# Down-bias sums of the first stage: from VectorE additions to TensorE identity products with ScalarE copies

## The reference, cut to what matters

```python
combine = combine.at[jnp.arange(N)[:, None], topk_idx].set(topk_w)
...
out = jnp.einsum('nei,edi->ned', act, down_proj) + down_proj_bias
y = jnp.einsum('ned,ne->nd', out, combine.astype(out.dtype))
...
x = x + _L0_attn_ref(xn, ...) + _L0_ffn_ref(xn, ...)
```

## Time and profile before

| | |
|---|---|
| median of 3 runs | 3066.34 us (3065.47 to 3067.68) |
| profiled execution, its time | 3062.34 us |
| profiled execution, its span | 3060.4 us |
| PE busy / PE weight loads busy | 2769.5 us / 2259.8 us |
| DVE, ACT, POOL busy | 2129.6, 1627.7, 1437.1 us |
| mean granted PE clock | 0.968 |

### The profile page before, as it was taken

One profiled execution on the slowest core, in us unless ns is written; L12 is line 12 of the kernel. 1 busy time (PEld: TensorE's weight loads), 2 busy tenths in 40 slices (PEclk: granted clock), 3 DMA queues, 4 the chain that ended last, 5 costly groups with the idle time before them and its releaser, 6 DMA issues. The chain is left out here.

```text
span 3060.4 us, 61227 instructions
## 1 busy us (share of the span) xinstructions
PE 2769.5 (90%) x20990; PEld 2259.8 (74%) x20990; DVE 2129.6 (70%) x6019; ACT 1627.7 (53%) x3420; POOL 1437.1 (47%) x2201
## 2 busy tenths in 40 slices
PE   5878799999999999979999999999799999999995
PEld 3655588898889889756666666666688888888864
DVE  5788788788778778767788888866544445444565
ACT  3555444544544444556656656665455555555563
POOL 4475843443453444365556665332333323333487
PEclk8888899999999999999999999999999999999998
DMA  3566678888789788422434443210566666566445
GB/s 84 203 233 241 219 278 296 293 296 309 280 290 325 276 296 309 153 45 54 100 99 108 110 111 105 95 70 26 210 228 208 211 204 238 204 215 208 138 89 127
DMA packets 212006, 580.12 MB, mean 190 GB/s; under 512 B 24616, under 2 KB 146416, under 8 KB 167408
## 3 DMA queue, kind: packets, MB, share of 16 engines
q1 hardware_dynamic: 172528, 523.82, 48.8%
q0 software_dynamic: 36864, 51.14, 8.2%
q10 hardware_dynamic: 2304, 1.21, 0.1%
HBM read 450.14 MB, written 125.96 MB: 188 GB/s over the span
## 5 line engine op out<-in xcount | busy, mean ns | idle before, releaser
L494 PE MATMUL bank<-xh,gu 128*128 128x256 f32 x3520 | 672.5, 291 | 34.2 <-DVE gc L1683 26.1
L1154 POOL TENSOR_TENSOR al<-t,ah 128x512 fp32r<-128x512 f32 x220 | 283.2, 1287 | 875.5 <-ACT ah L1388 875.5
L494 PEld LDWEIGHTS bank<-xh,gu 128*128 128x128 f32 x3520 | 512.4, 190 | 58.5 <-issue 55.6
L1885 DVE TENSOR_REDUCE st<-bank 128x1 f32<-128x512 f32 (+3 forms) x1024 | 421.9, 481 | 152.8 <-PE bank L555 146.5
L537 PE MATMUL bank<-masks_bf,ident_bf 128*128 128x128 bf16 x1896 | 428.2, 249 | 101.8 <-DVE st L1885 38.0
L1485 ACT ACTIVATE pt<-bank 128x512 f32<-128x512 f32 (+1 forms) x1152 | 509.4, 543 | 19.0 <-PE bank L558 17.5
L555 PE MATMUL bank<-ksT,qsT 128*128 128x512 f32 (+3 forms) x1536 | 408.7, 368 | 5.7 <-DVE top L1883 2.9
L537 PEld LDWEIGHTS bank<-masks_bf,ident_bf 128*128 128x128 bf16 x1896 | 168.7, 98 | 303.5 <-DVE st L1885 96.4
L1493 ACT ACTIVATE oT<-bank 128x512 f32<-128x512 f32 x192 | 114.5, 596 | 503.0 <-PE bank L634 499.7
L558 PE MATMUL bank<-qaT,ksT 128*128 128x512 f32 (+3 forms) x1536 | 381.9, 364 | 0.0
L1388 ACT ACTIVATE ah<-t 128x512 fp32r<-128x512 f32 x220 | 138.9, 631 | 399.6 <-DVE t L1709 358.5
(11 more groups left out here) (257 smaller groups left out, 5137.7 us busy)
## 6 DMA issues: line engine op xcount, KB each, us to landing
gu<-wu_scratch SPq DMA_DIRECT2D x110, 1032.0 KB, 5.1
gu<-wu_scratch SPq DMA_DIRECT2D x110, 1024.0 KB, 7.4
dn<-wd_scratch SPq DMA_DIRECT2D x110, 1024.0 KB, 6.7
xs<-xs_scratch SPq DMA_DIRECT2D x110, 264.0 KB, 4.3
ys_scratch<-yb SPq DMA_DIRECT2D x110, 256.0 KB, 7.0
raw<-in_gu SPq DMA_DIRECT2D x16, 1024.0 KB, 5.7
wu_scratch<-hi SPq DMA_DIRECT2D x16, 1024.0 KB, 5.2
wu_scratch<-lo SPq DMA_DIRECT2D x16, 1024.0 KB, 10.7
```

Of the source, the lines that this page charges most:

```text
L494: mm = pe.matmul(bank[:, TS * h:TS * (h + 1)], gu[:, col:col + P], x[s % 2][:, TS * k:TS * (k + 1)], start=(n == 0), stop=(n == len(terms) ...
L1154: pool.tensor_tensor(em["al"][s % 2][:, m, :], em["t"][g % 2][:, :], em["ah"][s % 2][:, m, :].bitcast(F32), ALU.subtract).then_inc(al_read ...
L1885: ins = dve.reduce_max(st[:, 0, r:r + 1], bank[:, first:first + width], AX.X)
```

## The change

PE now adds the rows itself: for each of the four 256-column quarters of a sequence it multiplies the 128 x 128 identity by the four-byte rows of `acc` (start of an accumulation) and adds the bias product to it (end of the accumulation). ScalarE copies the sums from the two banks back to `acc` (`take_biased`), and VectorE's two additions with the wait behind them go. The banks are now released by ScalarE. VectorE waits once in a sequence, in `context_out`, for the copy of that sequence, which was made many pairs earlier.

```diff
                     for i in range(2):
-                        bank = take(f"Rb{b}.{i}", "dve")
+                        bank = take(f"Rb{b}.{i}", "act")
                         for t in (2 * i, 2 * i + 1):
-                            mm = pe.matmul(bank[:, D * (t % 2):D * (t % 2 + 1)], ro["combT"][:, P * t:P * (t + 1)],
-                                           ro["db"][:, :], start=True, stop=True)
+                            to = bank[:, D * (t % 2):D * (t % 2 + 1)]
+                            pe.matmul(to, ident[:, :], acc[:, NT * b + t, :], start=True, stop=False)
+                            mm = pe.matmul(to, ro["combT"][:, P * t:P * (t + 1)], ro["db"][:, :], start=False, stop=True)
                         mm.then_inc(x_full, 1)
...
+                def take_biased(b):
+
+                    for i in range(2):
+                        act.wait_ge(x_full, X.full(f"Rb{b}.{i}"))
+                        act.activation(acc[:, NT * b + 2 * i:NT * b + 2 * i + 2, :],
+                                       X.bank(f"Rb{b}.{i}")[:, :].rearrange("p (t d) -> p t d", t=2),
+                                       ACT.Copy).then_inc(x_act, 1)
...
                     if routes(G, -1):
                         route_rows((G + 1) // 2)
+                    if routes(G, 3):
+                        take_biased((G - 3) // 2)
...
                 def context_out(n):
 
+                    dve.wait_ge(x_act, X.count[f"Rb{n}.1"])
...
-                def add_bias(b):
-
-                    for i in range(2):
-                        a = acc[:, NT * b + 2 * i:NT * b + 2 * i + 2, :]
-                        dve.wait_ge(x_full, X.full(f"Rb{b}.{i}"))
-                        dve.tensor_tensor(a, a, X.bank(f"Rb{b}.{i}")[:, :].rearrange("p (t d) -> p t d", t=2),
-                                          ALU.add).then_inc(x_dve, 1)
-                    dve.wait_ge(x_dve, X.count[f"Rb{b}.1"])
...
-                    if routes(G, 3):
-                        add_bias((G - 3) // 2)
```

## The result

The changed kernel takes 3087.62 us (median of four runs, 3086.09 to 3090.97), the kernel before beside it 3065.9 (median of four). The ratio on record is 1.0085 with an interval of 1.007 to 1.0099; these two medians alone give 1.0071, the low end. It is slower by 21.7 us where the forecast said 3.7, and the time lies outside the range.

The account below looks back on a forecast made before the run. In the first 380 us waits between engines decide, GpSimd's queue setting the end from pair 13; +4.4 us at its start, +0.5 behind, less a little for the clock, made about +4: 3070 us, range 3061 to 3078.

Parts of the forecast that it names:

- So depth costs nothing and I take 1.9 or 3.7 us: PE's four added identity products per sequence: priced like the 8-row bias products, 1.9 us at full clock, 3.7 at half.
- the terms of pairs 3 to 11: Shifts from PE's added products and removed wait: +1.9 in pair 3, -1.8 in 5, +1.8 in 7, +1.9 in 9 and 11.
- the sum at GpSimd's start: Start of GpSimd's stack in pair 13: six pair terms together make it +4.4 us later.
- the cover behind it: After pair 13 GpSimd's queue hides PE's delay: 5.4 us of delay against 4.55 us that PE waits for GpSimd.
- The clock suffers: Rival, chance 0.17: added columns run at half clock where it was low and the rise comes later; +14.8 us, 3081.
- the clock stays up: Rival, chance 0.25: full-depth identity products keep PE's clock high in the first 380 us; -4.9 us, 3061.4.
- Pair 13: Without DVE's additions, its head norms and the GpSimd start they release come 1.3 us earlier.
- Behind pair 13: Up to the first expert load: PE's uncovered delay and GpSimd's two short waits for PE add +0.5 us together.
- PE's waits at the third transpose: Pairs 5, 7, 13: PE no longer waits for DVE's addition; worth at most 2.14 us in 5, 0.68 in 7.
- ScalarE's copies: 16 copies of 0.60 us from the banks, covered by PE's work: taken as costing nothing.
- DVE's additions: 16 additions of 680 ns go, 10.9 us in all; nothing gained in pairs 3, 9, 11, 17.
- DVE's idle time before the maxima: Sign in pairs 3, 9, 11: longer than 6.48, 5.73, 3.45 us by 1.3 + 1.9.

Follow-up runs that it names:

- grouped: The changed kernel with a sequence's four identity products first, then its four bias products, sums wrong; 3055.63 us, 0.9981 of the kernel before.
- deep_before: The kernel before with its bias products made 128 rows deep by zero rows; 3091.74 us, 0.9974, and 0.9977 on a third chip.
- deep: The changed kernel with bias products padded by zero rows, so all products are 128 deep; 3052.44 us, 0.9972 of the kernel before, later 0.9967.
- act_only: The changed kernel without the identity products, ScalarE still copying, rows of x missing from the sums; 3055.65 us, 0.9985 of the kernel before.
- deep_pe_only: The kernel before with identity products added but overwritten, all products 128 rows deep, VectorE still adding; 3098.01 us, 0.9997 of the kernel before.
- pe_only: The kernel before with four identity products a sequence added but overwritten by the bias products, VectorE still adding; 3087.67 us, 1.0092 of the kernel before.

## Why the prediction was wrong

**The price of the products.** The step that failed is "So depth costs nothing and I take 1.9 or 3.7 us", on which the terms of pairs 3 to 11 rest, five of the six in the sum at GpSimd's start, and the cover behind it. It compared products 8 deep among themselves with products 128 deep among themselves, which is right (`grouped`: 1.90 us, `deep_before`: 1.97 and 3.76), and then put the two in turns. A full sequence of eight takes 4.98 us at full clock and 9.25 at half instead of 3.8 and 7.4. The rule that I leaned on, the Trainium skill, "TensorE: Matmul & The Clock Gate", in its part on the weight load, says that the row count doesn't matter for the time of that load. The trace agrees (at their fastest the loads of L734 take 186 ns and those of L735 181), but I took it for the price of the product in its place, and the depth decides when the load begins. The price stood in the trace of before, on a row that I didn't read: where the projections follow the bias products in pair 3, the weight load of the kernel before already waits.

```profile
106.68 0.50 PEld L581 LDWEIGHTS bank<-w_mla,xT 128*128 128x128 f32 x2 [0.65 <-issue]
```

The kernel before has one such stop at each sequence's end; the changed kernel has eight. The depth also changes ahead of the bias products, behind the router products of 8 columns, and there the loads of L733 waited once, 0.2 us, in the whole trace: behind a product that short there is hardly anything to wait for.

**The clock.** "The clock suffers" had 0.17 and was priced with the same products, at +14.8; of its mechanism much came true. The granted clock in the stretch is 0.80 where it was 0.84. Between the changed kernel and `deep` the eight stretches differ by 24.7 us (57.5 less 32.8 in the table). Of the 56 stops inside them 27 are of the half clock (0.65 us idle) and 29 of the full (0.33), which is 13 us at 0.29 and 0.18 from start to start; the other 12 us are work at half clock that `deep` does at full. The rival "the clock stays up" came true in `deep` (0.89) and in `grouped` (0.88), not in the changed kernel. So the objection raised against it, that half of the stream is still 8 rows deep, wasn't the reason: half of the stream of `grouped` is too. What `grouped` doesn't have is the alternation.

**Place by place**, predicted and as the two profiled executions have it. Seen is the later start of the first maxima behind the products (of GpSimd's stack in pair 13), as an increase over the changed pair before; 0.5 us of shift were there ahead of pair 3:

| pair | 3 | 5 | 7 | 9 | 11 | 13 | sum |
|---|---|---|---|---|---|---|---|
| predicted | +1.9 | -1.8 | +1.8 | +1.9 | +1.9 | -1.3 | +4.4 |
| seen | +4.8 | +1.35 | +4.0 | +4.0 | +8.0 | +2.3 | +24.6 |

The maxima of pair 7 in the kernel before, which no row above shows:

```profile
181.37 3.47 DVE L1885 TENSOR_REDUCE st<-bank 128x1 f32<-128x512 f32 x8 [0.96 <-PE bank L555]
```

Pair 13 went wrong in sign: DVE's head norms do end earlier relative to its pair, but GpSimd is now released by PE, which is so late that it sets GpSimd's start too. I had named DVE as releaser there and not asked how near behind PE was: its third transpose ended at 276.88, 1.5 us ahead of GpSimd's start. Behind pair 13 the forecast was +0.5, and the shift at the first load, 26.1 us, is 1.1 more than at GpSimd's stack. GpSimd's queue still set the end, but the 4.55 us by which it covered PE were used up: from 280 to 395 us PE of the changed kernel no longer waits for GpSimd's stack.

**What was right.** PE's waits at the third transpose went, ScalarE's copies cost nothing (`act_only` 0.9985), DVE's additions and PE's wait for them are worth about 4 us, added columns without stops cost 6.3 us at an equal clock (`deep_pe_only` less `deep_before`), no more than the prediction gave them, DVE's idle time before the maxima grew, and the later stages passed the shift on.

**Slips in the prediction.** The terms of "the clock stays up" add to -4.8, not -4.9, and behind pair 13 the sum shows 0.9 where +0.5 was taken. Neither decides anything.

**What stays open.** Why the loss is 0.85% in the first comparison, 0.92% in `pe_only` and 0.48% on the third chip; the kernel before itself differs by 1.3% between chips. The clock goes along with it: beside the kernel before on its chip `pe_only` lost 0.002 of mean granted clock (0.964 against 0.966), and the changed kernel on the third chip less than 0.001 (0.9595 against 0.9602). Why it is granted so is not shown. Why `deep_before` gains 7 us: one stop in each of eight sequences went, some 2 us in all (8 x 0.18 to 0.29), and the mean granted clock rose on both chips, from 0.960 to 0.966 and to 0.965. A rise of 0.005 is some 30 us less at half clock, by estimate up to 15 us of PE's work, so the clock is large enough to be the cause; the rows looked at here don't say where it was gained. And what exactly the clock follows.

## What to carry to other kernels

Price an added product in its place: the row before it and the row behind it have to be like it, and a product 8 or 64 rows deep among products 128 deep cost a stop on each side, unless the product ahead was very short. Other pairs of depths were not tried. Where products of different depth have to stand together, fill the shallow operand with zero rows: here that cost no time on PE (1.97 us against 1.99 for the bias products) and turned a loss of 0.85% into a gain of 0.28%, by the stops and by the clock together. Before a release is moved forward in a sum, look at who would release next.

## What the hardware showed that was not expected

- A change of depth between two products of 256 columns held the weight load back until the product before was all but through: idle for 0.65 us at half clock and 0.33 at full, 0.29 and 0.18 us from start to start. 64 beside 128 rows does as 8 beside 128 does.
- With as many columns and no stops, products 8 deep went with a granted clock of 0.77 from 100 to 380 us and products 128 deep with one of 0.85. Making the bias products 128 deep, with zero rows, raised the mean granted clock of the whole span from 0.960 to 0.966 and 0.965 on two chips (`deep_before`). The same products in turns and grouped, on one chip, went with 0.964 and 0.9725 (`pe_only`, `grouped`).
- One and the same kernel took 3059.65, 3099.37 and 3099.96 us on three chips, and what a change was worth differed too (1.0085 and 1.0048).
